# Cross-attention of a perceiver layer: probability sums on GpSimd down to two tiles per batch, one round of denominators, weight differences on VectorE

## The reference, cut to what matters

```python
def _layer_cut(Q, K, ...):              # Q = layernorm(x): (8, 64, 512), K = context: (8, 1601, 512)
    C_q = Q @ Wq_d;  C_kv = K @ Wkv_d   # 64 and 32 features
    CqWqk = (C_q @ W_qk).reshape(b, n, 16, 32)
    scores = einsum('bnhl,bkl->bhnk', CqWqk, C_kv) / sqrt(32)
    attn = softmax(scores, axis=-1)
    V_up = (C_kv @ Wv_u).reshape(b, 1601, 16, 32)
    out = einsum('bhnk,bkhd->bnhd', attn, V_up)

def _binary_diff_weight(w, base):       # for w1, w3, w2 of the third part
    d = w - base
    coeff = mean(abs(d))
    return base + coeff * sign(d)
```

## Time and profile before

| | |
|---|---|
| median of 3 runs | 978.36 us (976.01 to 979.28) |
| the profiled execution | 976.39 us, its span 974.6 us |
| mean granted TensorE clock | 0.964 |
| busy, whole span | PE 92%, PEld 67%, DVE 63%, ACT 52%, POOL 41% |
| cross-attention | about 35 to 318 us of the span, eight steps |

### The profile page before, as it was taken

The page is one execution under the profiler, slowest core; times in us unless marked ns, Lnnn a source line. Parts: engine busy times, 40 slices in busy tenths (PEclk is TensorE's granted clock), DMA queues, the critical chain, the costliest instruction groups (busy, mean ns, idle before and its releaser), DMA issues. The chain is left out here.

```text
span 974.6 us, 15256 instructions
## 1 busy us (share of the span) xinstructions
PE 900.9 (92%) x5298; PEld 653.6 (67%) x5298; DVE 618.2 (63%) x994; ACT 508.8 (52%) x995; POOL 402.8 (41%) x264
## 2 busy tenths in 40 slices
PE   4868999999998879999999999999999997599997
PEld 2334455545453658888888888888888886488886
DVE  3453567656671538767577675757757575688883
ACT  2315666666665546636365463645636364355551
POOL 3025778777876024323234232333323231344430
PEclk9857999999999889999999999999999999799999
DMA  9374765642440721111010110101101000465521
GB/s 331 128 257 185 276 258 210 241 157 96 153 143 2 259 76 44 45 33 49 20 51 22 43 43 22 43 22 43 43 22 43 12 1 1 153 206 201 194 90 43
DMA packets 46178, 103.70 MB, mean 106 GB/s; under 512 B 11314, under 2 KB 16434, under 8 KB 45106
## 3 DMA queue, kind: packets, MB, share of 16 engines
q1 hardware_dynamic: 44754, 102.94, 30.8%
q10 hardware_dynamic: 1376, 0.13, 0.2%
HBM read 97.08 MB, written 1.05 MB: 101 GB/s over the span
## 5 line engine op out<-in xcount | busy, mean ns | idle before, releaser
L1336 POOL TENSOR_TENSOR head_probs<-head_probs,inverse_den 128x576 f32<-128x576 f32 x128 | 147.0, 1148 | 298.3 <-DVE inverse_den L1267 298.2
L813 DVE TENSOR_REDUCE max_part<-psum 128x1 f32<-128x804 f32 x128 | 120.9, 989 | 57.7 <-PE psum L618 57.7
L745 ACT ACTIVATE probs<-psum 128x512 f32<-128x512 f32 (+1 forms) x208 | 107.9, 601 | 51.8 <-PE psum L639 47.4
L1214 ACT ACTIVATE head_probs<-psum,neg_max 128x576 f32<-128x576 f32 x128 | 94.6, 739 | 76.6 <-PE psum L1105 43.0
L536 POOL TENSOR_TENSOR prob_sums<-probs 128x1024 f32<-128x1024 f32 x48 | 114.4, 2389 | 26.2 <-PE psum L669 14.0
L1280 DVE TENSOR_REDUCE neg_max<-psum 128x1 f32<-128x576 f32 x128 | 96.1, 754 | 36.2 <-PE psum L1089 28.2
L1260 DVE TENSOR_TENSOR probs_t_low<-psum,probs_t_high 128x512 fp32r<-128x512 f32 x128 | 87.5, 684 | 9.0 <-ACT probs_t_high L1220 7.9
L618 PE MATMUL psum<-c_t,q_t 96*128 96x402 f32 x256 | 80.2, 402 | 11.7 <-DMA c_t<-c_high 7.3
L1089 PE MATMUL psum<-k_high,query_t_high 128*128 (+1 forms) x256 | 84.1, 329 | 5.0 <-DVE query_t_low L1245 2.9
L618 PEld LDWEIGHTS psum<-c_t,q_t 96*128 96x128 f32 x256 | 47.0, 206 | 58.0 <-DVE max_part L813 30.7
L1104 PE MATMUL psum<-ident,head_probs 128*128 128x128 f32 x512 | 78.3, 275 | 5.7 <-DVE mixed_t_low L1305 3.9
(11 more groups left out here) (160 smaller groups left out, 1914.4 us busy)
## 6 DMA issues: line engine op xcount, KB each, us to landing
cache<-in_ctx_dram SPq DMA_DIRECT2D x4, 3202.0 KB, 11.5
ctx_t_odd<-in_ctx_dram SPq DMA_DIRECT2D x4, 3202.0 KB, 11.4
w_raw<-in_L_ffn_w_dram SPq DMA_DIRECT2D x24, 448.0 KB, 5.1
w_raw<-in_L_ffn_mean_w_dram SPq DMA_DIRECT2D x24, 448.0 KB, 6.1
ffn_raw<-in_L_ffn_w_dram SPq DMA_DIRECT2D x42, 256.0 KB, 3.8
ffn_raw<-in_L_ffn_mean_w_dram SPq DMA_DIRECT2D x42, 256.0 KB, 4.1
wq_nat<-in_L_attn_wq_dram SPq DMA_DIRECT2D x32, 256.0 KB, 2.7
wo_nat<-in_L_attn_wo_dram SPq DMA_DIRECT2D x32, 256.0 KB, 2.6
```

Of the source, the lines that this page charges most:

```text
L745: act.activation(prob_buffer(b, t)[0:rows, half * BANK:(half + 1) * BANK], psum[0:rows, n % SCORE_BANKS, :], ACT.Exp, scale=XSCALE).then_i ...
L813: dve.tensor_reduce(max_part[:, qt, pair:pair + 1], psum[:, bank:bank + 2, 0:PIECE_KEYS], AX.XY, ALU.max).then_inc(s_max, 1)
L1214: act.activation(probs[:, qt, :].rearrange("p (a k) -> p a k", a=2), psum[:, 2 * (qt % 2):2 * (qt % 2) + 2, 0:HALF], ACT.Exp, bias=neg_max ...
L1336: pool.tensor_tensor(probs[:, qt, :], probs[:, qt, :], rden[:, qt:qt + 1].to_broadcast([P, KEYS]), ALU.mult).then_inc(s["norm"], 1)
```

## The change

GpSimd now adds the six pair tiles down to two, `sums[0]` (pairs 0 to 3) and `sums[4]` (pairs 4, 5 and the tail), with four more additions of 128x1024 per batch, 11 in all. `denominators` waits for all 11 and makes one round of four matmuls. GpSimd's differences go to VectorE, all three at the end of a step, behind `negate_max` and before `add_mixed`, `place_values` and `copy_u`. ScalarE sums piece 0 of the next batch at a step's end, and pieces 1 and 2 of the batch itself after tiles 3 and 7 of its own step. SyncE's loads move to fit: piece 0 of batch b - 1 behind the context of round b, pieces 1 and 2 at the head of the next round, and the last three before the gather; batch 1's loads no longer stand behind the second context.

```diff
-DIFF_AT = (0, 1, 2)
-ABS_AT = 3
+ABS_AT = {3: 1, 7: 2}
+POOL_ADDS = 11
+ADDED = (1, 2, 4, 5, 8, 9, 11)
...
     def pairs_summed(b, t):
...
-        return (g // KT) * (ADDS + 1) + (g % KT) // 2 + 1 if g >= 0 else 0
+        return (g // KT) * POOL_ADDS + ADDED[(g % KT) // 2] if g >= 0 else 0
...
                 if b > 2:
-                    load_pieces(b - 1, 1)
-                    load_pieces(b - 1, 2)
+                    load_pieces(b - 2, 1)
+                    load_pieces(b - 2, 2)
                 place_keys(b)
                 if b + 2 < BATCH:
                     sp.wait_ge(s_c, b + 1)
                     load_context(core, ctx_t, sp, b + 2, b % 2)
-                if b == 1:
-                    load_pieces(1, 0)
-                    load_pieces(1, 1)
-                    load_pieces(1, 2)
-                elif b > 1:
-                    load_pieces(b, 0)
-            load_pieces(BATCH - 1, 1)
-            load_pieces(BATCH - 1, 2)
+                if b > 1:
+                    load_pieces(b - 1, 0)
+            load_pieces(BATCH - 2, 1)
+            load_pieces(BATCH - 2, 2)
+            for i in range(3):
+                load_pieces(BATCH - 1, i)
...
+            def add_sums(b, n, into, other):
+
+                pool.wait_ge(s_add, POOL_ADDS * b + n)
+                pool.tensor_tensor(sums[into][:, :], sums[into][:, :], sums[other][:, :], ALU.add).then_inc(s_add, 1)
...
                 for u in range(ADDS):
-                    if u in DIFF_AT and s + 1 < BATCH:
-                        difference(s + 1, DIFF_AT.index(u))
                     add_pair(s, u)
+                    if u % 2:
+                        add_sums(s, ADDED[u], u - 1, u)
+                    if u == 3:
+                        add_sums(s, ADDED[u] + 1, 0, 2)
...
-                for k in range(ADDS // 2):
-                    pe.wait_ge(s_add, (ADDS + 1) * b + (2 * k + 2 if k < ADDS // 2 - 1 else ADDS + 1))
-                    for half in range(2):
-                        for odd in range(2):
-                            at = 2 * LKV * half + LKV * odd
-                            mm = pe.matmul(psum[at:at + LKV, DEN_BANK, :], ones[:, :],
-                                           sums[2 * k + odd][:, half * BANK:(half + 1) * BANK],
-                                           start=(k == 0), stop=(k == ADDS // 2 - 1))
+                pe.wait_ge(s_add, POOL_ADDS * (b + 1))
+                for half in range(2):
+                    for odd in range(2):
+                        at = 2 * LKV * half + LKV * odd
+                        mm = pe.matmul(psum[at:at + LKV, DEN_BANK, :], ones[:, :],
+                                       sums[4 * odd][:, half * BANK:(half + 1) * BANK], start=True, stop=True)
...
-                    if t == ABS_AT and b + 1 < BATCH:
-                        abs_sum(b + 1, 0)
+                    if t in ABS_AT and b > 0:
+                        abs_sum(b, ABS_AT[t])
...
                 if b + 1 < BATCH:
-                    abs_sum(b + 1, 1)
-                    abs_sum(b + 1, 2)
+                    abs_sum(b + 1, 0)
...
             place_values(1)
+            for i in range(3):
+                difference(0, i)
...
                 if lead:
                     negate_max(b + 1)
+                    for i in range(3):
+                        difference(b + 1, i)
```

More of the change, by code:

```diff
@@ L525, in _ @@
         def _(pool):
[L526 to L530, removed]
             def add_pair(b, u):
@@ L537, in add_pair @@
                                    ALU.add).then_inc(s_add, 1)
+            def add_sums(b, n, into, other):
+                pool.wait_ge(s_add, POOL_ADDS * b + n)
+                pool.tensor_tensor(sums[into][:, :], sums[into][:, :], sums[other][:, :], ALU.add).then_inc(s_add, 1)
             def add_tail(b):
                 pool.wait_ge(s_exp, HALVES * (b + 1))
-                pool.wait_ge(s_add, (ADDS + 1) * b + ADDS)
-                pool.tensor_tensor(sums[ADDS - 1][0:TAIL, :], sums[ADDS - 1][0:TAIL, :],
+                pool.wait_ge(s_add, POOL_ADDS * b + POOL_ADDS - 1)
+                pool.tensor_tensor(sums[4][0:TAIL, :], sums[4][0:TAIL, :],
                                    prob_buffer(b, KT - 1)[0:TAIL, :], ALU.add).then_inc(s_add, 1)
@@ L555, in _ @@
                     compressed_low(1)
-                    for i in range(3):
-                        difference(0, i)
                     continue
                 for u in range(ADDS):
-                    if u in DIFF_AT and s + 1 < BATCH:
-                        difference(s + 1, DIFF_AT.index(u))
                     add_pair(s, u)
+                    if u % 2:
+                        add_sums(s, ADDED[u], u - 1, u)
+                    if u == 3:
+                        add_sums(s, ADDED[u] + 1, 0, 2)
                     if s == 0 and u == 0:
@@ L820, in negate_max, with difference @@
                                   negate=True).then_inc(s_neg, 1)
+            def difference(k, i):
+                dve.wait_ge(s_raw[i], 32 * (k + 1))
+                dve.tensor_tensor(w_raw[:, i, 0, :], w_raw[:, i, 0, :], w_raw[:, i, 1, :],
+                                  ALU.subtract).then_inc(s_diff, 1)
             def place_values(b):
```

## The result

The changed kernel takes 1035.18 us (median of 4 runs, 1028.96 to 1040.48) against 977.18 for the kernel before in the same rounds: 1.059 times as long, 95% interval 1.053 to 1.066. Slower was right; 1007 was too low, and so was the end of the range, 1024. The profiled execution took 1028.96 us with a span of 1027.2, 52.6 more than before, and its mean granted clock was 0.917 against 0.964.

What follows compares the result with a forecast made beforehand. The prediction took TensorE to set the steps; from 976.4 us, 8.8 (steps 1 to 4), 6.0 (steps 5 and 6), 7.1 (step 7), 4.4 (step 0) and 5.0 (clock) add 31.3, stated as 1007 us, range 991 to 1024.

Steps and rivals of the forecast that it cites:

- part 1: Denominators on TensorE: one round instead of three saves 1.71 us in each of 8 steps, nothing in the last batch.
- parts 2 and 3: GpSimd's four more additions, alternating with VectorE's three differences at a step's end: steps 1 to 4, +8.8 us.
- Rival (a): At a step's end GpSimd keeps the lock, so difference 0 waits for the tail addition: 1021 us, chance 0.17.
- Rival (b): The lock doesn't matter, GpSimd and VectorE overlap or miss each other: 988 us, 983 if the clock holds; chance 0.12.
- Step 0: First step: batch 1's later loads delay the differences and move the denominators from 114.21 to 120.2: +4.4 us.
- Step 7: Last batch: ten additions in a row end at A + 26.8, the last round formerly began at 19.7: +7.1 us.
- Steps 5 and 6: Steps without values to place: the tail ends at A + 29.2 and the round follows, +3.0 us each.
- A: Start of a batch's first pair addition on GpSimd, used as the mark of each step.
- Later steps get their loads in time: SyncE's loads after step 0: a context and the pieces need 18.1 of 32 us.
- The clock: TensorE's clock falls in step 0's wait, +2.8 us, and before the last round, +2.2 us: +5.0 together.
- rival (c): The clock falls in the wait of each of steps 1 to 6 too, 2.8 us each: 1024 us, chance 0.12.

Runs made afterwards that it cites:

- e6: Changed kernel with 9 additions and two rounds in steps 0 to 4, absolute sums all in the next step, batch 1's loads early: 971.63 us, ratio 0.996.
- e9: The four-sum version (9 additions, two rounds) with a step's six weight loads issued before its context load instead of behind it: 968.03 us, ratio 0.994.
- e4: Changed kernel with filler matmuls of constants before each denominator wait, and more in step 0 before the copied latents: 1014.09 us, ratio 1.039.
- e3: Changed kernel with VectorE's differences replaced by a maximum over one weight half alone, one SBUF input, same waits and signals: 1001.50 us, ratio 1.026.
- e5: Changed kernel with batch 1's six weight loads back behind the second context: 1024.40 us, ratio 1.049.
- e10: Changed kernel with 7 additions and three rounds in the last batch alone: 1028.31 us, ratio 1.050.
- e1: Changed kernel's moved differences, loads and absolute sums, but 7 additions and three rounds as in the kernel before: 995.98 us, ratio 1.019.
- e11: Eleven additions and one round in steps 0 to 4 of the better order with early loads, plus filler matmuls before those denominators: 986.50 us, ratio 1.012.

## Why the prediction was right and wrong

- **One round saves 1.71 us (part 1): right, where it can be seen.** Two rounds for three give 0.87 a step, half of it, in e6 and e9. In the changed kernel nothing of it is left, since TensorE is no longer last.
- **Eleven additions and the turns (parts 2 and 3, +8.8): right.** The assumption that the engines alternate decided this sum, and the rows show it: 3.20 and 3.09 us. e4 gives +8.9 with the clock held. That the two sums agree so closely is luck in part: in e4 steps 1 and 3 grew by 1.5 and not 1.9, steps 2 and 4 by 3.0 and not 2.5, where the addition to x meets `compressed_low` on GpSimd and takes 1.6 us, not the 0.55 forecast. Rival (a), GpSimd keeping the lock, falls: the first absolute sum starts at 219.28, before the tail. Rival (b) falls with the same row and, since e3 without a lock is still 1.026, would not even have brought its 988.
- **Step 0 (+4.4, and 2.8 of clock): near,** +4.3 (the prediction's own terms give 4.3 too: 120.2 - 114.21 - 1.71), though the prologue ended 0.85 earlier, so the step itself took 5.2 more. The clock fell as forecast, near 112, but cost this step little; its half-speed start fell to step 1. e5 shows that the late loads are the cause.
- **Step 7 (+7.1): near,** +9.0, of which e10 puts 2.5 on the clock (22.2 against 19.7) and 6.5 on the four additions. The round and the mix at half clock cost 1.7, forecast 2.2.
- **Steps 5 and 6 (+3.0 each): the order was right, the clock was missing,** +6.8. "The tail ends at 29.2, the round follows" holds: e4 has the tail at A + 28.9 and 29.0. In the changed kernel it ends near A + 31.9, after a first 7.7 us at half clock. The chain difference 0, absolute sum, shift row, scores, which I had left out, does not end last with eleven additions; it makes the idle time in which the clock falls. With 7 additions, in e1, it does end last.
- **"Later steps get their loads in time": right here,** the changed kernel's differences wait for weights in step 0 alone (10.2 us in all). It doesn't hold for shorter steps: step 2 of e1, e3 and e6 waits for weights behind a context and takes 3.0, 4.6 and 3.6 us longer than step 1.
- **The clock (+5.0): the step that failed.** I let it fall once in step 0 and once at the end, and gave rival (c), a fall in each of steps 1 to 6, 0.12 at 2.8 us each. It fell at the end of every step. And a fall cost more, about half of the time that the next step then spends at half clock:

```
step                          1     2     3     4     5     6
over the forecast, us       4.5   4.4   0.6   6.6   3.8   3.8
of it at 1.2 GHz, us       10.5   7.9   1.4  13.0   7.7   7.7
half of that                5.3   4.0   0.7   6.5   3.8   3.8
```

The second row is the step's time from A until the clock is back; its half is an estimate of what half speed costs where TensorE is busy. So even (c), 1024 and the end of my range, was too low. The 2.8 came from the earlier trace rows, a stretch of 6 us of which half was lost. I took that as the length of every fall. Against rival (c) stood only that the clock stayed at 1.00 in the steps of before, where no wait was as long: but the forecast itself had made such waits, TensorE through at about A + 27.4 and the denominators at A + 31.0. The account: forecast without clock 26.3, steps 51.8. Of the missing 25, e4 returns 21 between the medians, and e11 18 in its pair; set against the kernel before in the same rounds it is 20 and 17.

The spread of the runs is 11.5 us here and 4.3 before. That the length of the slow stretches varies from execution to execution is seen in e10; that it makes the whole spread is an assumption, no run isolates it.

The Trainium skill (TensorE: Matmul & The Clock Gate, Part 1: The HAM clock gate) has the lower clock come with idleness and the higher one return under sustained work. The fall agrees with the rows of 224 to 226. The return is the open point: here it comes only after 15 us in which TensorE is marked busy nearly throughout, and the measurement decides. The same skill (SBUF — State Buffer, Who interferes with whom) lets whoever issues first have the shared port for its whole instruction; the alternating rows agree.

What stays open: why the clock took 7 us to return in one step and 17 or 20 in another.

## What to carry to other kernels

When you take work off the engine that sets the time by giving it to helpers, write out the helpers' order at the stage's end, lock turns included, and check that the last of them still comes before the bounding engine is through: nine additions did (0.994), eleven did not (1.059 as changed, 1.030 in the better order). A wait of 2 to 4 us on TensorE costs itself and, through the clock, up to 6.6 us more in the next step (0.6 to 6.6 here): price it so, and test it with matmuls of constants in the wait. Put such fillers where TensorE idles; behind the idle time they only make the step longer, as in steps 5 and 6 of e4. And an average that fits (27.0 of 30.3 us) says nothing about the last stage of a pipeline, where no next step hides the extra work.

## What the runs showed of the hardware

- Two queued streams, a 128x896 VectorE operation with both inputs in SBUF and 128x1024 GpSimd additions, take turns one instruction at a time, and the wait is shown inside the instruction: 3.20 us for 1.09, 3.09 for 2.38. With one input from SBUF a reduction keeps 1.08 beside the same additions, and a 64x256 TENSOR_TENSOR its 0.42.
- The clock falls in an idle stretch of 2.6 us (223.6 to 226.2) and is back only at about 241, although TensorE is marked busy in between; over the seven falls it is down for 7 to 20 us. The eight instructions of the denominators take 1.94 us instead of 1.07.
- The order of loads in one queue can decide by several microseconds: the weights ahead of the context instead of behind it take step 2 from 33.04 us (e6) to 29.46 (e9).
